# TensorE's product with w3 ahead of the values' product in six of eight slots of an attention and mixture-of-experts kernel

## The chip, the cores and the metric

One core of a Trainium2 chip runs the whole program. The metric is the device time of one execution in microseconds (us). TensorE (PE in the rows, with PEld for its weight loads), VectorE (DVE), ScalarE (ACT), GpSimd (POOL) and SyncE (SP, which only issues DMAs) each run a queue of their own, in order, and wait for each other on semaphores.

## The reference

For each of 8 batches, `x` is 256 x 128. All is in float32.

```python
def layer(x, ctx):                                   # x: (8, 256, 128), ctx: (8, 256, 64)
    n = layernorm(x)
    q, k, v = heads(n @ Wq + bq), heads(n @ Wk + bk), heads(n @ Wv + bv)     # 16 heads of 8
    y = softmax(causal(q @ k.T / sqrt(8))) @ v
    qc, kc, vc = heads(n @ Wcq + bcq), heads(ctx @ Wck + bck), heads(ctx @ Wcv + bcv)
    y = y + softmax(qc @ kc.T / sqrt(8)) @ vc
    x = x + merge(y) @ Wp + bp
    f = layernorm(x)
    shared = (silu(f @ w1.T) * (f @ w2.T)) @ w3s.T                           # hidden width 512
    scores = sigmoid(f @ router.T)
    gates = scores * top2_mask(scores + expert_bias)                         # 8 experts
    h1, h2 = split(einsum('td,ehd->teh', f, w12))                            # hidden width 128 each
    return x + shared + einsum('teh,edh->td', silu(h1) * h2 * gates, w3)
```

## The kernel before, in words

A batch's attention is cut into 8 *units*, each of 4 heads: units 0 to 3 are the causal self-attention, units 4 to 7 the attention to the context. A unit's softmax goes in four steps. TensorE computes the scores a first time, in two halves (`maxima`, lines 471, 472 and 476), and VectorE reduces them to maxima (lines 1057 and 1063). TensorE transposes the maxima into the bank Y (`shift_rows`, line 549) and VectorE subtracts them from the queries (`qs`, line 1030). TensorE computes the shifted scores in two halves (`exp_pass`, lines 458 and 460) and ScalarE exponentiates them into `probs` (line 816). Last comes the *values' product* (`values`, line 582), 16 matmuls of `vs` with `probs` into Y, which ScalarE copies into `yT` (line 803).

The feed-forward part is cut into 6 *pairs* of chunks (2 pairs of the shared expert, 4 of the routed ones). For a pair TensorE computes h1 into bank A and h2 into bank Bk (`hidden`, line 434, which is also the line of other products), ScalarE takes the tanh (`th`, line 796), VectorE makes `act` (line 939) and `hid` (`times_h2`, line 948, which reads h2 out of Bk). Then comes the *product with w3* (`w3_product`, line 434, `Bk<-w3T,hid`, 8 matmuls), written over h2 in Bk, and VectorE adds the result to `acc` (`add_up`, lines 963 and 979).

The program is written out in turns. Turn t runs t from -1 to 7 through 8 *slots*, and a written-out list (`DRAIN`) of what is left follows. Slot s of a turn works on several units at once: the exponential pass is that of unit s, `shift_rows` that of the next unit, `maxima` that of the unit after, `values` that of the unit before. Six slots also carry a pair of an earlier batch:

```python
def pair_of(s):
    return {5: (0, -1), 6: (1, -1), 0: (2, -2), 1: (3, -2), 2: (4, -2), 3: (5, -2)}.get(s)
```

The second number says how many turns back the pair's batch lies. So turn 1 has pairs in slots 5 and 6 only, and turns 2 to 7 have them in all six: 38 in the turns and 10 in the drain, which calls `values` and `w3_product` from its own list.

What happens in a slot with a pair, in the order of each engine's queue:

- TensorE: exponential pass half 0, half 1 (which wait for the reduced maxima of the next unit, half 0 and half 1, since they write over those scores), h1, h2, an early use of bank Cb, `shift_rows`, maxima half 0 and half 1 (which wait for ScalarE's exponentials of the slot, half 0 and half 1), then the two products in question, then a late use of bank Cb. The late uses are `tokens2` in slot 0 (transposes of `yT`, line 665, which wait for the copy of unit 7 that the same slot's values' product feeds), the q and k projections in 1, the output projection in 2, `x2T` in 3, `cT` in 4 (a slot with no pair), the router in 5, none in 6 and `tokens1` in 7 (no pair either). In slots 3 and 4 short matmuls that only keep TensorE busy (`fill`, line 490) stand ahead of the exponential passes.
- VectorE: `act`, `qs` of the next unit (waits for `shift_rows`), `hid`, the maxima half 0 and half 1, `add_up` (waits for the product with w3), and what it has to do for bank Cb.
- ScalarE: exponentials half 0, the tanh, exponentials half 1, what it has to do for the early use of Cb, the copy to `yT` (waits for the values' product), the late use of Cb.

`values` waits for Y to be free, which it is when VectorE has finished `qs`, and for `probs`. `w3_product` waits for `hid`.

Of the kernel before, what the change touches and what calls it, by code (L numbers as in the profile page):

```python
# [45 lines left out]
def values_of(s):  # L46
    return ((s - 1) % SLOTS, 0 if s > 0 else -1)


def pair_of(s):  # L50
    return {5: (0, -1), 6: (1, -1), 0: (2, -2), 1: (3, -2), 2: (4, -2), 3: (5, -2)}.get(s)


def h1_of(s):

    return {4: (0, -1), 5: None, 7: (2, -1), 0: None}.get(s, pair_of(s))
# [78 lines left out]
def wait(eng, sem, n):  # L135

    if not isinstance(n, int) or n > 0:
        eng.wait_ge(sem, n)
# [20 lines left out]
def attention_moe_program(nc, x, ctx_in, Wk, bk, Wq, bq, Wv, bv, Wck, bck, Wcq, bcq, Wcv, bcv, Wp, bp,  # L159
                          w12, w3, shared_w1, shared_w2, shared_w3, router_w, expert_bias, out):  # L160
    with ExitStack() as stack:
# [162 lines left out]
        def wait_bank(eng, turn, uses, free, name):  # L324

            found, wrapped = turn.users_before(uses, name)
            if uses is C_USES and turn.at(-1):
                found = found[1:2]
            elif uses is C_USES and turn.at(0) and wrapped:
                found = found[0:2]  # L330
            else:
                found = found[0:1]
            for before, off in found:
                s, part, of = free[before]
                wait(eng, s, turn.n(off, part, of))
# [12 lines left out]
        def raw_banks(turn, s):  # L348

            if turn.at(0):  # L350
                return [s] if s < SLOTS - 1 else []
            return [SLOTS - 1 + s] if turn.at(1) and SLOTS - 1 + s < RAW_BANKS else []
# [77 lines left out]
        def _(pe):  # L430
            def parts(dst, pairs_):

                for i, (a, m) in enumerate(pairs_):
                    mm = nc.tensor.matmul(dst, a, m, start=(i == 0), stop=(i == len(pairs_) - 1))  # L434
                return mm
# [51 lines left out]
            def fill(bank, n):  # L487

                for _ in range(n):
                    nc.tensor.matmul(bank[:, 0:T], ident_bf[:, :], causal[:, :].unsqueeze(1).broadcast_to([P, 2, P]),  # L490
                                     start=True, stop=True)
# [13 lines left out]
            def exp_pass(turn, s):  # L505

                if turn.has(0):
                    for half in range(2):
                        if half == 0:

                            wait(pe, shifted[s], turn.n(0))
                        keep_warm(turn, s, WARM_EXP)
                        un, on = shift_of(s)
                        if turn.has(on):

                            wait(pe, reduced[un], turn.n(on, half + 1, 2))
                        else:
                            wait(pe, exped[s - 1], turn.n(0, half + 1, 2))
                        exp_scores(s, half).then_inc(scores[s], 1)

            def hidden(turn, pair, w, i=0):

                p, o = pair
                if w == 0 and p == 0:
                    wait(pe, x2T_hi, turn.n(o))
                    wait(pe, x2T_lo, turn.n(o))
                if w == 0 and p == 0 and turn.at(1):
                    pe.wait_ge(raw_hi, RAW_BANKS)
                    pe.wait_ge(raw_lo, PAIRS)
                if w == 1 and i == 0:  # L530

                    if p > 0:
                        wait(pe, summed[p - 1], turn.n(o, SUM_STEPS[p - 1], SUM_STEPS[p - 1]))
                    elif turn.loop or turn.t + o > 0:
                        wait(pe, summed[PAIRS - 1], turn.n(o - 1, SUM_STEPS[-1], SUM_STEPS[-1]))
                bank = pair_banks[i % SETS][w]
                for c in range(2):
                    mm = parts(bank[:, c * T:(c + 1) * T],
                               three(w12_hi[:, p, w, c, :], w12_lo[:, p, w, c, :], x2T[:, 0, :], x2T[:, 1, :]))
                mm.then_inc(ffn[p], 1)  # L540

            def shift_rows(turn, s):

                u, o = shift_of(s)
                if turn.has(o):
                    wait(pe, reduced[u], turn.n(o, 2, 2))
                    wait_bank(pe, turn, Y_USES, y_free, f"shift{u}")
                    for qt in range(NT):
                        mm = nc.tensor.transpose(Y[:, qt * P:(qt + 1) * P], shifts[:, qt, :], ident[:, :])  # L549
                    mm.then_inc(shift_T[u], 1)  # L550
# [17 lines left out]
            def values(turn, s):  # L568

                u, o = values_of(s)  # L570
                if turn.has(o):
                    wait_bank(pe, turn, Y_USES, y_free, f"value{u}")
                    wait(pe, exped[u], turn.n(o, 2, 2))
                    if u < NG:
                        wait(pe, masked[u], turn.n(o))
                    kind, g = divmod(u, NG)
                    if g == 0:
                        wait(pe, v_ready[kind], turn.n(o))
                    for kt in range(NT):
                        for j in range(GH):  # L580
                            q0 = P * kt if kind == 0 else 0
                            mm = nc.tensor.matmul(Y[QUAD * j:QUAD * (j + 1), q0:T], vs[:, kind, kt, GH * g + j, :],  # L582
                                                  probs[u % 2][:, j, kt * T:(kt + 1) * T - q0],
                                                  start=(kt == 0), stop=(kt == NT - 1))
                    mm.then_inc(valued[u], 1)

            def w3_product(turn, pair, i=0):

                p, o = pair
                wait(pe, hid_ready[p], turn.n(o))  # L590
                bank = pair_banks[i % SETS][1]
                if p < SHARED_PAIRS:
                    for tt in range(NT):
                        mm = parts(bank[:, tt * P:(tt + 1) * P],
                                   [(hid[i % SETS][:, c, tt * P:(tt + 1) * P], w3T[:, 2 * p + c, :]) for c in range(2)])
                else:
                    for c in range(2):
                        for tt in range(NT):
                            k = c * NT + tt
                            mm = parts(bank[:, k * P:(k + 1) * P],  # L600
                                       [(hid[i % SETS][:, c, tt * P:(tt + 1) * P], w3T[:, 2 * p + c, :])])
                mm.then_inc(ffn[p], 1)
# [81 lines left out]
            def one_turn(turn):  # L684
                for s in range(SLOTS):
                    exp_pass(turn, s)
                    if pair_of(s):
                        if h1_of(s) and turn.has(h1_of(s)[1]):
                            hidden(turn, h1_of(s), 0)
                        if s == 6:  # L690
                            bank_c(turn, EARLY[s])
                        if turn.has(pair_of(s)[1]):
                            hidden(turn, pair_of(s), 1)
                        if turn.at(1) and s == 2:

                            fill(Bk, 3)
                        if s != 6:
                            bank_c(turn, EARLY[s])
                        shift_rows(turn, s)
                        for half in range(2):  # L700
                            maxima(turn, s, half)
                        values(turn, s)
                        if turn.has(pair_of(s)[1]):
                            w3_product(turn, pair_of(s))
                    else:
                        shift_rows(turn, s)
                        maxima(turn, s, 0)
                        if turn.has(h1_of(s)[1]):
                            hidden(turn, h1_of(s), 0)
                        bank_c(turn, EARLY[s])  # L710
                        maxima(turn, s, 1)
                        values(turn, s)
                    for i in raw_banks(turn, s):
                        raw_bank(i)
                    bank_c(turn, LATE[s])

            def drain(turn):
                for step, i in DRAIN:
# [18 lines left out]
                    elif step == "bank_c":  # L737
                        bank_c(turn, (i, -1))

            turns(pe, one_turn, drain)  # L740


# [482 lines left out]
```

## Time and profile before

| | |
|---|---|
| time before, median of 3 runs | 424.03 us (423.29 to 424.42) |
| the profiled execution, its own time | 421.15 us |
| its span in the trace | 419.4 us |
| TensorE busy (matmuls) | 385.7 us, 92% |
| TensorE's weight loads | 291.9 us, 70% |
| VectorE busy | 352.0 us, 84% |
| ScalarE busy | 197.4 us, 47% |
| GpSimd busy | 77.5 us, 18% |
| DMA | 47 GB/s on average |

The span is the stretch that the trace covers; 1.7 us of the execution's time lie outside it. Times in the rows are microseconds from the start of the span. The end of a matmul in the trace is modelled, so the starts are the safer numbers. A bracket behind a row gives the idle time of the engine just before it and who ended it.

### The profile page before, as it was taken

To read this page: it belongs to the slowest core of one execution; us is meant where nothing else is said; L and a number is where in the kernel's file an instruction comes from. 1 tells how busy PE (TensorE), PEld (TensorE's weight loads), DVE (VectorE), ACT (ScalarE), POOL (GpSimd) and SP (SyncE) were. 2 spreads that over 40 slices of the span, in tenths; PEclk is the share of its full clock that TensorE was granted. 3 is DMA by queue.
4 is the path that set the end of the run, shared out by engine and by line. 5 is a ranking of instruction groups with operands and counts; after the bars stand their busy time and mean duration, and the time that the engine had idled before them with its cause. 6 is when DMAs were issued, how large, how long until landed. Compare 5 with 4: busy or idle time off the path is not lost.

```text
span 419.4 us, 10085 instructions
## 1 busy us (share of the span) xinstructions
PE 385.7 (92%) x3724; PEld 291.9 (70%) x3724; DVE 352.0 (84%) x1186; ACT 197.4 (47%) x326; POOL 77.5 (18%) x140
## 2 busy tenths in 40 slices
PE   1569999999999999999999999999999999999996
PEld 0446666667687767867687767867787767767895
DVE  4487777787999889998999889988999789884897
ACT  5125655555453554554454554554454554455221
POOL 5012101312122012212132013212131103201210
PEclk9999999999999999999999999999999999999999
DMA  5721102010201102110111101110201101000000
GB/s 129 222 101 45 65 19 90 34 45 20 71 19 58 52 20 70 52 46 12 65 33 52 52 33 57 59 52 2 77 15 45 45 33 46 2 27 1 2 15 13
DMA packets 28496, 19.87 MB, mean 47 GB/s; under 512 B 6680, under 2 KB 26272, under 8 KB 28448
## 3 DMA queue, kind: packets, MB, share of 16 engines
q1 hardware_dynamic: 27296, 19.02, 14.0%
q8 instruction: 30, 0.49, 0.5%
q10 hardware_dynamic: 1152, 0.20, 0.3%
q14 instruction: 18, 0.15, 0.1%
HBM read 5.58 MB, written 1.05 MB: 16 GB/s over the span
## 4 chain that ended last, share of the span: by engine, by line
PE 62%; DVE 26%; issue 6%; ACT 2%; DMA 2%; SPq 1%; DVEq 0%; ACTq 0%
PE Bk L434 12%; PE Y L582 9%; PE A L434 8%; DVE shifts L1063 7%; PE S L458 7%; PE Cb L434 7%; DVE masked_s L1057 5%; PE S L476 3%; PE Y L549 3%; PE Cb L665 3%; PE S L471 2%; DVE hid L948 2%; DVE act L939 2%; PE S L460 2%; DVE acc L979 2%
## 5 line engine op out<-in xcount | busy, mean ns | idle before, releaser
L816 ACT ACTIVATE probs<-S 128x1024 f32<-128x1024 f32 (+1 forms) x128 | 114.1, 916 | 45.6 <-PE S L460 44.8
L1057 DVE CUSTOM_DVE_ANT_0 masked_s<-S,later_keys 128x256 f32<-128x256 f32 (+1 forms) x256 | 74.1, 353 | 5.1 <-PE S L472 4.9
L1063 DVE TENSOR_REDUCE shifts<-S 128x4 f32<-128x1024 f32 x64 | 75.4, 1217 | 0.9 <-PE S L476 0.5
L803 ACT COPY yT<-Y 128x256 f32<-128x256 f32 x64 | 23.8, 373 | 94.6 <-PE Y L582 94.6
L582 PE MATMUL Y<-probs,vs 128*32 128x256 f32 (+1 forms) x1024 | 62.4, 361 | 3.9 <-DVE qs L1030 2.9
L1113 POOL TENSOR_SCALAR_AFFINE_SELECT probs<-probs 128x1024 f32<-128x1024 f32 x32 | 35.2, 1101 | 154.0 <-ACT probs L816 154.0
L458 PE MATMUL S<-qs,qk 32*128 32x256 f32 x256 | 45.4, 387 | 7.7 <-DVE shifts L1057 4.5
L434 PEld LDWEIGHTS Bk<-w3T,hid 128*128 128x128 f32 x336 | 40.7, 191 | 12.6 <-DVE hid L948 8.5
L434 PE MATMUL Bk<-w3T,hid 128*128 128x128 f32 x336 | 48.4, 287 | 0.6 <-DVE hid L948 0.6
L582 PEld LDWEIGHTS Y<-probs,vs 128*32 128x32 f32 x1024 | 26.9, 110 | 25.4 <-DVE qs L1030 8.8
L1030 DVE TENSOR_TENSOR qs<-qk,Y 128x256 fp32r<-128x256 f32 x64 | 26.6, 415 | 18.5 <-PE Y L549 18.5
L458 PEld LDWEIGHTS S<-qs,qk 32*128 32x128 f32 x256 | 22.9, 184 | 25.8 <-issue 8.6
L939 DVE SCALAR_TENSOR_TENSOR act<-th,A 128x512 f32<-128x512 f32 x42 | 28.7, 683 | 11.7 <-ACT th L796 11.1
L796 ACT ACTIVATE th<-A 128x512 f32<-128x512 f32 x42 | 25.2, 599 | 24.6 <-PE A L434 24.5
L434 PE MATMUL A<-x2T,w_hi 128*128 128x256 f32 x168 | 36.1, 307 | 0.0
L434 PE MATMUL Bk<-x2T,w_hi 128*128 128x256 f32 x168 | 34.0, 295 | 0.0
L979 DVE SCALAR_TENSOR_TENSOR acc<-Bk,gates,acc 128x128 f32<-128x128 f32 x112 | 31.3, 341 | 0.2 <-PE Bk L434 0.2
L460 PE MATMUL S<-qs,qk 32*128 32x128 f32 (+1 forms) x256 | 30.5, 249 | 0.0
L549 PE MATMUL Y<-ident,shifts 128*128 128x128 f32 x128 | 26.9, 292 | 2.6 <-DVE shifts L1057 2.6
L948 DVE TENSOR_TENSOR hid<-act,Bk 128x512 f32<-128x512 f32 x42 | 28.6, 681 | 0.5 <-PE Bk L434 0.4
L434 PEld LDWEIGHTS A<-x2T,w_hi 128*128 128x128 f32 x168 | 25.4, 188 | 4.2
L434 PEld LDWEIGHTS Bk<-x2T,w_hi 128*128 128x128 f32 x168 | 25.6, 188 | 2.6 <-issue 0.4
(149 smaller groups left out, 679.8 us busy)
## 6 DMA issues: line engine op xcount, KB each, us to landing
qk<-nat SPq DMA_DIRECT2D x192, 64.0 KB, 1.9
xin<-in_x_dram SPq DMA_DIRECT2D x8, 128.0 KB, 2.3
w_raw<-in_L_ffn_w_dram SPq DMA_DIRECT2D x4, 256.0 KB
xres<-in_x_dram SPq DMA_DIRECT2D x8, 128.0 KB, 2.4
out_dram<-acc SPq DMA_DIRECT2D x8, 128.0 KB, 1.8
cin<-in_ctx_dram SPq DMA_DIRECT2D x8, 64.0 KB, 2.1
w_raw<-in_L_ffn_shared_w_dram SPq DMA_DIRECT2D x4, 128.0 KB
w_raw<-in_L_ffn_w_dram SPq DMA_DIRECT2D x1, 512.0 KB
```

The source lines that it names most:

```text
L434: mm = nc.tensor.matmul(dst, a, m, start=(i == 0), stop=(i == len(pairs_) - 1))
L458: nc.tensor.matmul(S[:, j, 0:T], qk[r, u, 1, 0:P], qs[r, u % 2, :], start=True, stop=True)
L460: mm = nc.tensor.matmul(S[:, j, T:2 * T - q0], qk[r, u, 1, P:T], qs[r, u % 2, q0:T], start=False, stop=True, skip_group_check=True)
L549: mm = nc.tensor.transpose(Y[:, qt * P:(qt + 1) * P], shifts[:, qt, :], ident[:, :])
L582: mm = nc.tensor.matmul(Y[QUAD * j:QUAD * (j + 1), q0:T], vs[:, kind, kt, GH * g + j, :], probs[u % 2][:, j, kt * T:(kt + 1) * T - q0], st ...
L816: nc.scalar.activation(probs[s % 2][:, hs, 0:kept(s)], S[:, hs, 0:kept(s)], ACT.Exp, scale=SCALE).then_inc(exped[s], 1)
L939: nc.vector.scalar_tensor_tensor(out=act1[i % SETS][:, :], in0=th[i % SETS][:, :], scalar=1.0, in1=pair_banks[i % SETS][0], op0=ALU.add, o ...
L948: nc.vector.tensor_tensor(hid[i % SETS][:, :, :].rearrange("p c t -> p (c t)"), act1[i % SETS][:, :], pair_banks[i % SETS][1], ALU.mult).t ...
L979: nc.vector.scalar_tensor_tensor(out=acc[:, tt, :], in0=bank[:, k * P:(k + 1) * P], scalar=gates[:, tt, e:e + 1], in1=acc[:, tt, :], op0=A ...
L1057: r_ = nc.vector.tensor_tensor_reduce(out=masked_s[:, j, T - q * T:T - q * T + keys], in0=S[:, j, T - q * T:T - q * T + keys], in1=later_k ...
L1063: nc.vector.tensor_reduce(dst.rearrange("p q j -> p j q"), S[:, hs, :].rearrange("p j (q k) -> p j q k", q=NT), AX_X, ALU.max).then_inc(re ...
L1113: return nc.gpsimd.affine_select(out=dst, in_=dst, compare_op=compare, fill=fill, base=base, pattern=pattern, channel_multiplier=step)
```

## The change

In the six slots with a pair, the two calls at the end of the slot's TensorE work trade places. The drain's list and all other engines' queues stay as they are.

```diff
@@ one_turn of TensorE
                         shift_rows(turn, s)
                         for half in range(2):
                             maxima(turn, s, half)
-                        values(turn, s)
                         if turn.has(pair_of(s)[1]):
                             w3_product(turn, pair_of(s))
+                        values(turn, s)
                     else:
                         shift_rows(turn, s)
                         maxima(turn, s, 0)
```

## Rows read from the trace of the kernel before

**Rows 1.** Busy time by engine in one whole turn.

```profile
232.79:279.64 46.85, 45.65 (x464) 34.85 (x460) 42.42 (x147) 23.36 (x39) 9.09 (x15) 1.00 0.14 45
```

**Rows 2.** The chain of work that ended last, slots 1 to 3: start, us, what.

```profile
261.38 1.09 PE Bk L434 x8
...
271.63 0.83 PE Cb L434 x6
```

**Rows 3.** Timeline, end of slot 5 and start of slot 6.

```profile
236.50 0.68 DVE L948 TENSOR_TENSOR hid<-act,Bk 128x512 f32<-128x512 f32 x1
236.63 1.07 PE L582 MATMUL Y<-probs,vs 128*32 128x256 f32 x16
239.89 0.19 PEld L458 LDWEIGHTS S<-qs,qk 32*128 32x128 f32 x2 [0.30 <-DVE shifts L1063]
```

**Rows 4.** Timeline, end of slot 6 and start of slot 7.

```profile
243.71 0.68 DVE L948 TENSOR_TENSOR hid<-act,Bk 128x512 f32<-128x512 f32 x1
243.84 1.07 PE L582 MATMUL Y<-probs,vs 128*32 128x256 f32 x16
245.93 0.39 PE L458 MATMUL S<-qs,qk 32*128 32x256 f32 x2
246.48 1.94 ACT L816 ACTIVATE probs<-S 128x1024 f32<-128x1024 f32 x2 [1.13 <-PE S L460]
247.65 0.33 PE L471 MATMUL S<-qk 32*128 32x128 f32 x2
```

**Rows 5.** Timeline, end of slot 0 and start of slot 1.

```profile
253.64 0.68 DVE L948 TENSOR_TENSOR hid<-act,Bk 128x512 f32<-128x512 f32 x1
253.94 1.07 PE L582 MATMUL Y<-probs,vs 128*32 128x256 f32 x16
254.94 1.16 PE L434 MATMUL Bk<-w3T,hid 128*128 128x128 f32 x8
255.07 0.37 ACT L803 COPY yT<-Y 128x256 f32<-128x256 f32 x1 [1.36 <-PE Y L582]
255.93 0.60 PE L665 MATMUL Cb<-ident,yT 128*128 128x128 f32 x4
256.92 0.19 PEld L458 LDWEIGHTS S<-qs,qk 32*128 32x128 f32 x2 [0.16 <-DVE shifts L1057]
```

**Rows 6.** Timeline, the two products of slot 1.

```profile
260.39 0.68 DVE L948 TENSOR_TENSOR hid<-act,Bk 128x512 f32<-128x512 f32 x1
260.53 0.86 PE L582 MATMUL Y<-probs,vs 128*32 128x256 f32 x16 [0.35 <-DVE qs L1030]
```

**Rows 7.** Timeline, the two products of slot 2.

```profile
266.31 0.68 DVE L948 TENSOR_TENSOR hid<-act,Bk 128x512 f32<-128x512 f32 x1
266.54 0.86 PE L582 MATMUL Y<-probs,vs 128*32 128x256 f32 x16
```

**Rows 8.** Timeline, end of slot 3 and start of slot 4.

```profile
273.21 0.68 DVE L948 TENSOR_TENSOR hid<-act,Bk 128x512 f32<-128x512 f32 x1
273.35 0.86 PE L582 MATMUL Y<-probs,vs 128*32 128x256 f32 x16
276.21 2.09 ACT L816 ACTIVATE probs<-S 128x1024 f32<-128x1024 f32 x2 [0.29 <-PE S L460]
276.73 0.39 PE L458 MATMUL S<-qs,qk 32*128 32x256 f32 x2 [0.24 <-DVE shifts L1063]
277.53 0.51 PE L476 MATMUL S<-qk 32*128 32x256 f32 x4
```

**Rows 9.** Timeline, exponential pass half 1 of slot 2 in turn 7.

```profile
356.59 0.19 PEld L458 LDWEIGHTS S<-qs,qk 32*128 32x128 f32 x2 [0.64 <-DVE shifts L1057]
```

**Rows 10.** Costliest groups of the page: busy us, mean ns, idle before.

```profile
L979 DVE SCALAR_TENSOR_TENSOR acc<-Bk,gates,acc 128x128 f32<-128x128 f32 x112 | 31.3, 341 | 0.2 <-PE Bk L434 0.2
```

**Rows 11.** Timeline, a values' product of the first turn.

```profile
34.11 1.51 PE L582 MATMUL Y<-probs,vs 128*32 128x256 f32 x16
```

## The prediction

> **What bounds the kernel now.** I read the page first (TensorE 92% busy, VectorE 84%), then the windows of one turn, then the chain of waits, and last the timeline of that turn around each of the six slots with a pair.
>
> One turn lasts 46.85 us, in which TensorE is busy for 45.65 and VectorE for 42.42 [rows 1]. Neither has room to spare: TensorE's idle time comes in pieces of a few tenths of a microsecond. The reader is to see in the chain that it runs on TensorE without a break from the product with w3 of slot 1 to the early product of slot 3, 261.38 to 272.46 us (23 pieces, all PE) [rows 2]. What delays TensorE there delays the kernel in full. Elsewhere the chain passes to VectorE for a while (maxima, `qs`, `hid`) and back.
>
> The reader is to see in each slot's timeline which of two products could start first. VectorE makes `qs` and right behind it `hid`. The values' product starts as soon as `qs` is done (in slot 1 after 0.35 us idle for it [rows 6]), and runs while `hid` is being made. The product with w3 needs `hid`.
>
> **The change part by part.** No instruction is added or taken away: 16 matmuls of the values' product and 8 of the product with w3, with their weight loads, change order. No DMA moves, since neither product issues one, and POOL and SP wait for neither.
>
> *What gets sooner.* The product with w3 ends sooner by at most the length of the values' product. Its only reader is `add_up`, which stands behind two maxima in VectorE's queue. Its 112 instructions for the routed pairs had 0.2 us of idle time ahead of them in all, for TensorE [rows 10]. So there is 0.2 us to win at most, and I count nothing.
>
> *What gets later.* TensorE now stands at the product with w3 until `hid` is done, with the values' product queued behind it, which could have run. The delay in each slot is the end of `hid`, plus 0.05 us for the signal, less the time at which the values' product started before. The 0.05 is an estimate, from the 0.06 us between the modelled end of a values' product and the copy that waits for it (253.94 + 1.07 = 255.01, and 255.07 [rows 5]).
>
> - Slot 5: 236.50 + 0.68 + 0.05 - 236.63 = 0.60 us [rows 3]
> - Slot 6: 243.71 + 0.68 + 0.05 - 243.84 = 0.60 [rows 4]
> - Slot 0: 253.64 + 0.68 + 0.05 - 253.94 = 0.43 [rows 5]
> - Slot 1: 260.39 + 0.68 + 0.05 - 260.53 = 0.59 [rows 6]
> - Slot 2: 266.31 + 0.68 + 0.05 - 266.54 = 0.50 [rows 7]
> - Slot 3: 273.21 + 0.68 + 0.05 - 273.35 = 0.59 [rows 8]
>
> *What of it lies beside other work.* The delay is worth nothing where TensorE would have waited anyway before the next thing that counts.
>
> Slot 5: half 1 of the next exponential pass had 0.30 us of idle time before it, for VectorE's maxima [rows 3]. These run beside the products and don't get later. The delay is 0.60 - 0.30 = **0.30**.
>
> Slot 6: the late slot is empty, and the exponential pass comes next. ScalarE had been idle for 1.13 us when the scores of half 0 came, and its two exponentials took 1.94, so 0.97 each. Half 0 ended near 247.45, and the maxima of slot 7 started at 247.65 [rows 4], because they wait for it. So the delay goes scores, exponentials, maxima, and no slack takes from it: **0.60**.
>
> Slot 0: the delay of the product with w3 is 0.43, but the late use here is `tokens2`, which reads the `yT` that this slot's values' product feeds. Before, the product with w3 stood between, and the copy (255.07 to 255.44) was done before the transposes (255.93), hidden below it [rows 5]. That cover is gone. The product with w3 starts at 254.37 and has the 0.99 us from 254.94 to 255.93, so the values' product starts at 255.36. The copy starts 1.13 behind that start as before (253.94 to 255.07), at 256.49, takes 0.37, and with the signal the transposes start at 256.91 and not 255.93, 0.98 later. Half 1 of the next exponential pass had 0.16 us of idle time before it, for VectorE [rows 5]: **0.82**.
>
> Slots 1 and 2 lie in the unbroken stretch of TensorE [rows 2]: **0.59** and **0.50** in full.
>
> Slot 3: half 1 of the next pass stood 0.24 us idle for VectorE [rows 8], which would leave 0.35. But the exponentials of half 0 started 0.29 us after ScalarE went idle, for the scores, took 1.04 each and ended at 277.25; the maxima of slot 4 started at 277.53 [rows 8]. With 0.59 more they end at 277.84. From the end of such an exponential to the maxima I take 0.09 us, between the 0.05 of a signal and the 0.20 of slot 6 (247.45 to 247.65 [rows 4]), so the maxima start at 277.93: **0.40**.
>
> The sum of a turn is 0.30 + 0.60 + 0.82 + 0.59 + 0.50 + 0.40 = **3.21 us**. Turns 2 to 6 have all of it: 16.05. Turn 1 has slots 5 and 6: 0.90. In turn 7 the pass behind slot 1 had 0.64 us idle before it, for VectorE [rows 9], which covers slot 1's 0.59: 2.62. The drain's order doesn't change: nothing. Together 19.6 us.
>
> *Bounds of what the trace doesn't show.* No matmul of the values follows one with w3 in the trace, and none of an exponential pass follows one of the values. From one group to the next the shape of the weights changes three times in a slot, before as after, so I take zero. The two groups differ little in length, start to next start: 1.00 us for 16 matmuls of values, 0.99 for 8 with w3 [rows 5]. As bounds I take a tenth of that, 0.1 us less or more in each of 38 slots, 3.8 us both ways. The slacks may overlap or be used twice: without any of them (0.30 + 0.16 + 0.19 in a turn, and 0.64 once) the sum is 4 us larger.
>
> The profiled execution took 421.15 us, so it becomes 440.7. The median of the runs shown, 424.03, is 2.9 us above it, so the runs should show 443.6.
>
> **The rivals.**
>
> *VectorE takes it up.* VectorE is busy for 42.42 of 46.85 us of a turn [rows 1]. If it sets the pace in more places than I read, only the delays in the unbroken stretch and at the copy count: 0.82 + 0.59 + 0.50 = 1.91 a turn, 12 us in all, **436**. For it speaks the chain's passing to VectorE in slots 3, 5 and 6; against it, that its `qs` there waits for TensorE's transposes, so it gets later with them.
>
> *Everything adds.* No slack counts, and the changes of shape cost 0.1 us more in each slot: 19.6 + 4 + 3.8 = 27.4 us, **451**. For it speaks that a late TensorE also starts VectorE's next maxima late; against it, that the idle times in the rows are there.
>
> *Not slower.* The whole delay hangs on `hid` being ready after the maxima's last matmul. Were it ready before the values' product started, that is 0.43 to 0.60 us sooner against TensorE than in these rows, the product with w3 would fill the time in which TensorE stood for `qs` (0.35 us in slot 1 [rows 6]), and slots other than slot 0 would cost nothing or win. A point for it would be that the later TensorE gives VectorE time to catch up. But `qs` is released by TensorE's own transposes and `hid` follows it, so they move together. It would give 424 less 0.3 for each of 32 slots, more 0.5 for each of 6 slots 0 (the 0.98 less 0.43, for the copy): about **418**.
>
> *The clock falls.* The granted clock was 1.00 in the turn read (the level of 2.4 GHz), with TensorE idle for 1.2 us of 46.85 [rows 1]; now it is idle for 4.4. A values' product took 1.07 us in this turn [rows 3] and 1.51 in the first one [rows 11]. If that is what the lower level costs, a turn's 45.65 us of TensorE's work would take 64.4, and a single turn that ran so would add 19 us: **462** or more. Against it: the `fill` matmuls stay, and no single pause here is longer than about 1 us. The Trainium skill (TensorE: Matmul & The Clock Gate, A second HAM failure mode) reports a kernel whose clock swung between its two levels because TensorE paused briefly and often between groups of matmuls. This change adds just such pauses, so by that rule this rival would be the likelier one; the trace shows short pauses in every slot and a clock that stayed up.
>
> **How the numbers follow.** My sum, 0.66, with 439 to 448 as its own range; VectorE takes it up 0.12; everything adds 0.14; not slower 0.04; the clock 0.04. The predicted time is 443.6 us. The range of 434 to 452 holds the first three, and leaves out the last two and the far ends. The runs of the kernel before lie 1.1 us apart, about 0.3%, so that much is what can be told from no change. Slower by more than that has 0.96; faster and within it share the case of not slower, 0.02 each.
>
> **What would show it.** In the profile after, the product with w3 should stand idle for `hid` (line 948) before its first matmul, on PE and not on PEld alone, some 0.5 to 0.8 us in nearly every slot: more than 15 us over the run, where the values' product had its small waits for `qs`. The transposes `Cb<-ident,yT` of slot 0 should wait 0.5 us for ScalarE's copy. A turn should last 50.1 us. `add_up` should start as soon behind the maxima as before. The prediction is wrong if a turn stays under 48 us, if the maxima's reductions start no later against the turn than now, or if the granted clock leaves 1.00.

## The result, and the profile after

The changed kernel takes 446.01 us (median of 5 executions, 442.94 to 454.25), against 424.03 us before (423.29 to 424.55): 1.052 times as long, with a 95% interval of 1.048 to 1.056. That is 22.0 us slower, where 19.6 were forecast, and inside the range.

Some executions of every kernel here, the one before included, have a mean granted clock below 0.998 and are 2 to 15 us longer than the others. So I compare two other numbers beside the medians. The first are the executions with a mean of 0.998 or more ("at full clock"): 442.94 and 443.31 us for the changed kernel, and 421.06 to 421.62 for the kernel before, taken beside the later experiments, so +21.8 us. The second is the length of one turn in the trace. The trace of the changed kernel is that of the execution of 454.25 us. Its granted clock was at the lower level in two stretches, of which the later one ends at 117.2 us, and stood at 1.00 in turns 2 to 7, which lie behind that.

The windows of one whole turn of the changed kernel, against [rows 1]:

```profile
223.88:274.22 50.34, 45.37 (x460) 34.17 (x460) 42.89 (x148) 22.99 (x39) 9.17 (x15) 1.00 0.13 44
```

The turn is 50.35 us long and not 46.85: 3.50 more, where the sum said 3.21. TensorE's busy time is about what it was (45.65 us before, 45.37 now), so its idle time has grown from 1.2 us to 5.0. The clock stayed at 1.00.

The page's costliest groups name the place; the second row answers to [rows 10]:

```profile
L434 PE MATMUL Bk<-w3T,hid 128*128 128x128 f32 x336 | 50.3, 294 | 23.8 <-DVE hid L948 23.6
...
L979 DVE SCALAR_TENSOR_TENSOR acc<-Bk,gates,acc 128x128 f32<-128x128 f32 x112 | 31.4, 344 | 0.2 <-PE Bk L434 0.2
```

TensorE stood 23.6 us for `hid` ahead of the product with w3, and `add_up` waits for TensorE exactly as long as before, 0.2 us. So what the swap makes sooner, nobody had waited for.

The timeline of the changed kernel at the ends of slots 5, 6, 0, 1, 2 and 3, against [rows 3 to 8]. The bracket is the idle time before, and who ended it.

```profile
259.12 1.16 PE L434 MATMUL Bk<-w3T,hid 128*128 128x128 f32 x8 [0.59 <-DVE hid L948]
260.21 1.07 PE L582 MATMUL Y<-probs,vs 128*32 128x256 f32 x16
...
266.55 1.16 PE L434 MATMUL Bk<-w3T,hid 128*128 128x128 f32 x8 [0.67 <-DVE hid L948]
...
277.07 1.16 PE L434 MATMUL Bk<-w3T,hid 128*128 128x128 f32 x8 [0.37 <-DVE hid L948]
278.15 1.07 PE L582 MATMUL Y<-probs,vs 128*32 128x256 f32 x16
279.29 0.37 ACT L803 COPY yT<-Y 128x256 f32<-128x256 f32 x1 [2.88 <-PE Y L582]
279.72 0.66 PE L665 MATMUL Cb<-ident,yT 128*128 128x128 f32 x4 [0.49 <-ACT yT L803]
...
284.50 1.16 PE L434 MATMUL Bk<-w3T,hid 128*128 128x128 f32 x8 [0.94 <-DVE hid L948]
285.59 0.86 PE L582 MATMUL Y<-probs,vs 128*32 128x256 f32 x16
286.38 0.50 PE L434 MATMUL Cb<-xT,wx_hi 128*128 128x256 f32 x2
...
291.10 1.16 PE L434 MATMUL Bk<-w3T,hid 128*128 128x128 f32 x8 [0.45 <-DVE hid L948]
...
298.70 1.16 PE L434 MATMUL Bk<-w3T,hid 128*128 128x128 f32 x8 [0.69 <-DVE hid L948]
```

All six places show the stand, 0.37 to 0.94 us. In slot 1 it was 0.35 for `qs` before [rows 6], and is 0.94 for `hid` now: 0.59 more, as worked out. In slot 0 the second stand is there too, 0.49 us for the copy of `yT`. One number is new: from the first matmul with w3 to the first of the values it takes 1.09 us (259.12 to 260.21, and 284.50 to 285.59), where w3's 8 matmuls and the group behind them were 0.99 apart in slot 0 before [rows 5], and 0.92 in slot 1:

```profile
261.31 1.16 PE L434 MATMUL Bk<-w3T,hid 128*128 128x128 f32 x8
262.23 0.48 PE L434 MATMUL Cb<-xT,wx_hi 128*128 128x256 f32 x2
```

To place the loss, I took the start of half 1 of each exponential pass (the fifth of a pass's eight weight loads `S<-qs,qk`) and the distance from one pass to the next. "Slot 0" is the distance from the pass of slot 0 to that of slot 1, and holds slot 0's two products. One turn, in us:

| slot | 0 | 1 | 2 | 3 | 4 | 5 | 6 | 7 | turn |
|---|---|---|---|---|---|---|---|---|---|
| before | 5.38 | 6.42 | 6.21 | 7.17 | 3.99 | 6.03 | 6.77 | 4.90 | 46.87 |
| after | 6.16 | 6.99 | 6.95 | 7.60 | 4.13 | 6.35 | 6.69 | 5.48 | 50.35 |

Turns 2 to 6 of the kernel before are 46.80 to 46.87 us long by this reading. I go on with the 46.85 of [rows 1], so a difference of turns is good to about 0.03 us. Part of slot 3's delay comes out one slot later (in 4), and all of slot 6's (in 7), by way of ScalarE's exponentials.

### The profile page after: what moved, and what is told of

It reads as the page before. It is cut to its first block, busy times and chain, and to the rows that moved or that the text cites. A ratio compares the mean times of both kernels' runs of the same rounds, so it can differ in the third digit from the quotient of the medians.

```text
span 452.5 us, 10085 instructions
## 1 busy us (share of the span) xinstructions
PE 396.5 (88%) x3724; PEld 296.6 (66%) x3724; DVE 355.0 (78%) x1186; ACT 195.7 (43%) x326; POOL 77.8 (17%) x140
## 3 DMA queue, kind: packets, MB, share of 16 engines
HBM read 5.58 MB, written 1.05 MB: 15 GB/s over the span
## 4 chain that ended last, share of the span: by engine, by line
PE 61%; DVE 23%; ACT 6%; issue 6%; DMA 2%; SPq 1%; DVEq 0%; ACTq 0%
PE Bk L434 15%; PE Y L582 12%; PE Cb L434 8%; PE A L434 6%; DVE hid L948 6%; PE S L458 5%; DVE masked_s L1057 4%; DVE act L939 3%; ACT probs L816 3%; PE S L476 2%; PE Y L549 2%; PE Cb L665 2%; ACT th L796 2%; PE S L460 2%; DVE qs L1030 1%
## 5 line engine op out<-in xcount | busy, mean ns | idle before, releaser
L434 PE MATMUL Bk<-w3T,hid 128*128 128x128 f32 x336 | 50.3, 294 | 23.8 <-DVE hid L948 23.6
L582 PE MATMUL Y<-probs,vs 128*32 128x256 f32 (+1 forms) x1024 | 65.0, 374 | 0.0
L434 PEld LDWEIGHTS Bk<-w3T,hid 128*128 128x128 f32 x336 | 42.3, 197 | 31.9 <-DVE hid L948 31.8
L458 PE MATMUL S<-qs,qk 32*128 32x256 f32 x256 | 38.9, 395 | 3.8 <-DVE shifts L1057 2.7
L434 PE MATMUL Bk<-x2T,w_hi 128*128 128x256 f32 x168 | 35.1, 302 | 0.0
L796 ACT ACTIVATE th<-A 128x512 f32<-128x512 f32 x42 | 25.1, 598 | 19.6 <-PE A L434 18.9
L458 PEld LDWEIGHTS S<-qs,qk 32*128 32x128 f32 x256 | 19.9, 189 | 20.7 <-issue 14.8
L476 PE MATMUL S<-qk 32*128 32x256 f32 x256 | 26.3, 336 | 0.7 <-ACT probs L816 0.2
```

Source lines behind the costliest of these rows:

```text
L458: nc.tensor.matmul(S[:, j, 0:T], qk[r, u, 1, 0:P], qs[r, u % 2, :], start=True, stop=True)
L476: mm = nc.tensor.matmul(S[:, j, q * T:(q + 1) * T], qk[r, u, 0, q * P:(q + 1) * P], qk[r, u, 1, :], start=(q == 0), stop=True, skip_group_ ...
L796: nc.scalar.activation(th[i % SETS][:, :], pair_banks[i % SETS][0], ACT.Tanh, scale=0.5).then_inc(ffn_th[p], 1)
```

## The experiments

Each kernel has the same work as the kernel before, in another order. The turn is read from the trace as in the table above, in turn 4.

### The swap in slot 0 alone

```diff
-                        values(turn, s)
+                        if s != 0:
+                            values(turn, s)
                         if turn.has(pair_of(s)[1]):
                             w3_product(turn, pair_of(s))
+                        if s == 0:
+                            values(turn, s)
```

> The product with w3 stands ahead of the values' product in slot 0 alone (6 places). The copy theory: slot 0 pays twice, for the wait on hid and for the copy to yT that is no longer hidden below the product with w3, 0.82 us a turn, so 424.0 + 4.9 = 428.9 us, and the transposes Cb<-ident,yT wait some 0.5 us for the copy. Rival, only the wait on hid costs: 0.43 - 0.16 = 0.27 a turn, 425.6. Rival, VectorE sets the pace there: 424.

Measured: 429.25 us (427.57 to 431.74, clock 0.980 to 0.995; none at full clock), a ratio of 1.011 with an interval from 0.998 to 1.023, which alone decides nothing. The turn decides: 47.57 us, so 0.72 more than before (0.79 more in slot 0, and 0.10 less in slot 1). That is near the copy theory (0.82), and neither 0.27 nor nothing. The timeline of this kernel at the end of slot 0:

```profile
215.10 1.16 PE L434 MATMUL Bk<-w3T,hid 128*128 128x128 f32 x8 [0.37 <-DVE hid L952]
216.19 1.07 PE L582 MATMUL Y<-probs,vs 128*32 128x256 f32 x16
217.32 0.37 ACT L807 COPY yT<-Y 128x256 f32<-128x256 f32 x1 [2.89 <-PE Y L582]
217.75 0.31 PEld L665 LDWEIGHTS Cb<-ident,yT 128*128 128x128 f32 x3 [0.97 <-ACT yT L807]
217.75 0.44 PE L665 MATMUL Cb<-ident,yT 128*128 128x128 f32 x2 [0.49 <-ACT yT L807]
```

The copy now lies between the two TensorE groups, with nothing beside it.

### The swap everywhere but in slot 0

The same diff with the two conditions turned round (`s == 0` and `s != 0`).

> The swap in slots 5, 6, 1, 2 and 3, and the old order in slot 0. My sum without slot 0: 19.6 - 4.9 = 14.7, so 438.7 us, with stands of 0.5 to 0.7 us before the product with w3 for hid. If slot 0 is what carries the loss (its copy), 428 or less. If delays add up or cancel between slots, this and the run with slot 0 alone won't sum to the whole loss of some 19 to 22 us.

Measured: 440.13 us (438.27 to 444.95); at full clock 438.27 and 438.53, so 17.1 us more than before, where 14.7 were expected. The turn is 49.64 us, 2.79 more. With slot 0's 0.72 that makes 3.51, the whole change's 3.50. So slot 0's loss and that of the others add up and neither hide nor feed each other, and it is the other slots' terms, not slot 0's, that were too small in sum.

### Slots 1 and 2; slots 3, 5 and 6

The same diff with `s in (1, 2)` and with `s in (3, 5, 6)`.

> The swap in slots 1 and 2 alone (12 places), where the chain of the kernel before ran on TensorE without a break. The wait for hid alone: 0.59 + 0.50 = 1.09 us a turn, less slot 1 in the last turn: 5.9 us. With a cost of the order itself, seen in the changed kernel's trace (1.09 us from the first matmul with w3 to the first of the values, against 0.92 to 0.99 from w3's first to that of the group behind it before), 0.1 to 0.17 more in each: 7.3 us over a run of before at full clock. Rival, VectorE sets the pace: 2 us or less.

> The swap in slots 3, 5 and 6 (20 places), where TensorE had idle time for VectorE behind the products. My sum with slack taken off: 0.40 + 0.30 + 0.60 a turn, 8.7 us in all, and with 0.17 for the order in slots 3 and 5 some 10.5 us. Rival, everything adds (no slack counts): 20 times 0.60, with the order's cost 14 us. Rival, VectorE takes it up: 4 us or less.

Measured for slots 1 and 2: 429.99 us (428.70 to 439.57; ratio 1.014, 1.010 to 1.018); at full clock 428.70 and 428.83, and a turn of 48.24, 1.39 more. None of the executions of the kernel before beside these two kernels was at full clock, so I set their times against the 421.06 to 421.62 of the other experiments: 7.4 us more. That is the wait plus the cost of the order (7.3), and more than the wait alone (5.9). The turn says it more firmly, since the wait alone would have been 1.09. For slots 3, 5 and 6: 432.13 us (430.50 to 441.69; ratio 1.019, 1.015 to 1.023); at full clock 430.50 and 431.22, 9.2 to 9.9 more, and a turn of 48.21, 1.36 more. That lies between my sum with and without the order's cost (8.7 and 10.5). Both rivals fall: slack counts (not 14), and VectorE doesn't take the delay up (not 4). The two turns add to 2.75, against 2.79 for the five slots together.

### VectorE makes `hid` ahead of `qs`, in the changed kernel and in the one before

```diff
+                    if pr and turn.has(pr[1]):
+                        times_h2(turn, pr)
                     u, o = shift_of(s)
                     if turn.has(o):
                         ...
                         nc.vector.tensor_tensor(qs[:, u % 2, :], ...)
-                    if pr and turn.has(pr[1]):
-                        times_h2(turn, pr)
```

> The changed kernel, and VectorE makes hid ahead of qs instead of behind it (no work added). The theory that TensorE's wait for hid is the loss: hid is ready 0.4 us sooner, or in slot 5 a whole microsecond, and the stands shrink from about 0.6 us to 0 to 0.3, so the time falls by more than half of the loss, to 427 to 434 us; slot 0 keeps its wait for the copy. Rival, the order itself costs on TensorE (a change of shape of weights between the groups, 0.1 us or more in each place): the time stays at 440 or above though the waits for hid are gone.

> The control: the kernel before with VectorE making hid ahead of qs. By the wait theory now the values' product stands for qs, which comes 0.4 to 0.68 us later in every slot but 5, so this is slower than before by some 10 to 18 us (434 to 442). If making hid first is good or bad by itself for another reason (VectorE's maxima), it would show here too: a time below 424 would say that the gain of the run beside it is not the wait for hid.

Measured for the changed kernel with `hid` first: 431.72 us (428.69 to 435.74; ratio 1.016, 1.011 to 1.021), 428.69 to 429.65 at full clock, and a turn of 48.10. No work was taken away and TensorE's new order stayed, only the wait got shorter, and 2.25 of the turn's 3.50 us are gone. The rival, that the order itself costs nearly all, falls. The timeline shows what is left in slot 2:

```profile
225.60 0.69 DVE L952 TENSOR_TENSOR hid<-act,Bk 128x512 f32<-128x512 f32 x1
226.21 0.41 DVE L1037 TENSOR_TENSOR qs<-qk,Y 128x256 fp32r<-128x256 f32 x1
226.35 1.16 PE L434 MATMUL Bk<-w3T,hid 128*128 128x128 f32 x8 [0.24 <-DVE hid L952]
```

The product with w3 starts while VectorE is still at `qs`, after 0.24 us and not 0.45.

The control, the kernel before with `hid` first, took 432.24 us (431.01 to 444.74; ratio 1.016, 1.003 to 1.029), 431.01 and 431.55 at full clock, and a turn of 48.34. Its table of waits has the mirror image of the stand (us in total, times, longest):

```profile
PE Y L582 <- DVE qs L1033: 20.6, 32, 1.5
```

TensorE stood 20.6 us for `qs` ahead of the values. So the direction is as expected: the product that goes first must be the one whose operand VectorE makes first. The size was not: 9.8 us at full clock lies just below the 10 to 18 expected. Slots 5 and 6 had got shorter by 0.47 and 0.26 us (5.56 and 6.51), which I had not counted. That pointed to the experiment with `hid` first in slot 5.

### The same, with slot 0 left as it was before

`hid` first and the swap, both with the condition `s != 0`.

> The changed kernel with hid made ahead of qs, but both orders of before in slot 0. The copy theory: slot 0's transposes no longer wait for the copy, which takes 0.5 us or more off each of 6 turns: 424 to 426 us at full clock against 428.7 with slot 0 changed. If slot 0 costs nothing once hid is early, 428.7 stays.

Measured: 427.48 us (426.41 to 432.90; ratio 1.007, 1.001 to 1.013), 426.41 to 426.51 at full clock. It is 2.2 us below the kernel with slot 0 changed; the turn is 47.67, 0.43 less: slot 0 is 0.54 shorter (5.37 against 5.91) and slot 1 0.11 longer. So the swap in slot 0 costs something even when `hid` is early, as the copy theory says. Its absolute time lies 0.4 us above what I expected.

### TensorE's late use of bank Cb ahead of the products

The third way to take the wait away: let TensorE do other work meanwhile, with VectorE's order untouched. First in the kernel before, in slot 1 only; then in slots 1, 2 and 5, with the swap everywhere; then with the swap in these three slots only.

```diff
+                        if late_first:                      # s == 1, or s in (1, 2, 5)
+                            bank_c(turn, LATE[s])
                         ...
-                    bank_c(turn, LATE[s])
+                    if not late_first:
+                        bank_c(turn, LATE[s])
```

> The kernel before with the q and k projections of slot 1 ahead of both products. They don't depend on qs, so TensorE has work in the 0.35 us in which it stood for qs there. The theory that order counts by what TensorE has ready: 0 to 0.3 us less in each of 5 or 6 turns, so 419.5 to 421 at full clock. If a change of shape between the groups eats it, no change or up to 1 us slower.

> The changed kernel with the late use of bank Cb (the q and k projections, the output projection, the router) ahead of both products in slots 1, 2 and 5. VectorE's order is not touched, so hid comes no sooner; TensorE has 0.45 to 0.9 us of other work while it is made. The wait theory: the stands for hid in these slots shrink to 0 to 0.15 us, and the turn falls from 50.35 to some 48.9 us, the whole by about 9 us, to 434 at full clock. Rival, the order's change of shapes is the loss: the turn stays above 50.

> Slots 1, 2 and 5 with the late use of bank Cb first, then the product with w3, then the values' product; slots 0, 3 and 6 as before. If both waits (for qs and for hid) are hidden and only the shapes cost 0.1 to 0.17 us a slot: a turn of 46.7 to 47.3 us against 46.85, 420 to 424 us at full clock. Under 46.8 it would beat the kernel before.

`late_first` took 428.69 us (426.00 to 431.51; ratio 1.012, 1.006 to 1.018), with the clock at 0.980 to 0.992 in all its executions; the turn is 46.84, the same as before. The 0.35 us of slot 1 weren't won:

```profile
267.19 0.47 PE L434 MATMUL Cb<-xT,wx_hi 128*128 128x256 f32 x2
...
268.06 0.86 PE L582 MATMUL Y<-probs,vs 128*32 128x256 f32 x16
268.85 1.16 PE L434 MATMUL Bk<-w3T,hid 128*128 128x128 f32 x8
269.94 0.39 PE L458 MATMUL S<-qs,qk 32*128 32x256 f32 x2
```

The product with w3 now has the exponential pass behind it, 1.09 us after its start, where the projections had come after 0.92. This order, too, has one change of weight shape more than the order before (four and not three, counted further down). From the first matmul of the maxima to the next exponential pass it took 3.44 us, where it had been 3.51, and half 1 of that pass came 0.07 us later behind half 0, so that nothing was left.

`late_first_after` took 452.91 us (450.96 to 463.77; ratio 1.072, 1.065 to 1.079), and its turn is 51.12 and not 48.9. I was wrong on the total, but the slots tell two things apart. Slot 1 went from 6.99 to 6.31 and slot 2 from 6.95 to 6.48. In `late_first_three`, where slot 0 is as before, they are 6.40 and 6.48 against 6.42 and 6.21 before. So slot 1's loss is gone in full and slot 2's by 0.47 of 0.74. This order takes away two things at once: the wait, which now has other work under it, and the added change of weight shape, since the late use and the product with w3 stand together again. It doesn't tell their shares apart. Slot 5 went the other way, to 8.26 and to 6.72 us:

```profile
255.28 0.35 PE L434 MATMUL Cb<-router_hi,x2T 128*128 128x8 f32 x2 [1.05 <-DVE vs L904]
...
255.94 1.83 PE L434 MATMUL Bk<-w3T,hid 128*128 128x128 f32 x8
257.70 1.94 PE L582 MATMUL Y<-probs,vs 128*32 128x256 f32 x16
```

The router's product needs bank Cb, which VectorE gives back only when it has made `vs`, and `vs` stands behind `hid` in its queue. I had overlooked that wait: instead of hiding the one for `hid`, the move put a longer one, 1.05 us, in its place. What it did to the clock stands further down. `late_first_three` took 434.29 us (431.77 to 438.39; ratio 1.028, 1.021 to 1.035), with a turn of 47.67 where 46.7 to 47.3 were expected, and is slower than the kernel before.

### `hid` first in slot 5 of the kernel before

The diff of above with the condition `s == 5`, and no swap.

> The kernel before with one thing changed: in slot 5 VectorE makes hid ahead of qs. There VectorE stood idle for 1.02 us before qs with act and h2 ready, so hid costs qs nothing, and the maxima behind it start up to 0.6 us sooner, for which the next exponential pass waited 0.30 us. With hid first in all slots the interval of slot 5 was 5.56 us against 6.03. If that gain belongs to slot 5 itself: a turn of 46.4 to 46.6 us instead of 46.85, some 2 us less in all. If it was only time borrowed from the slots before, the turn stays at 46.85.

Measured: 421.33 us (417.84 to 431.80) against 423.37 beside it, a ratio of 0.991 (0.986 to 0.997); at full clock 417.84 to 418.29 against 421.18 to 421.62, 3.4 us less, where some 2 were expected. The turn is 46.23 us, 0.62 less (46.4 to 46.6 were expected), of which slot 5 gives 0.48. In the kernel before VectorE had stood idle in slot 5 ahead of `qs`:

```profile
236.16 0.42 DVE L1030 TENSOR_TENSOR qs<-qk,Y 128x256 fp32r<-128x256 f32 x1 [1.02 <-PE Y L549]
```

With `hid` moved into this gap, the timeline is:

```profile
233.69 0.69 DVE L948 TENSOR_TENSOR hid<-act,Bk 128x512 f32<-128x512 f32 x1 [0.24 <-PE Bk L434]
234.48 0.42 DVE L1033 TENSOR_TENSOR qs<-qk,Y 128x256 fp32r<-128x256 f32 x1
...
234.95 1.07 PE L582 MATMUL Y<-probs,vs 128*32 128x256 f32 x16
235.21 2.35 DVE L1066 TENSOR_REDUCE shifts<-S 128x4 f32<-128x1024 f32 x2
237.61 0.40 PE L458 MATMUL S<-qs,qk 32*128 32x256 f32 x4
```

The maxima follow `qs` after 0.73 us, where 1.33 us lay between the two starts before (236.16 to 237.49), and the exponential pass no longer waits for them: its four matmuls stand in one row. This version is faster than both kernels, if only by 0.9% than the one before.

### The swap from turn 2 on

```diff
-                        values(turn, s)
+                        if turn.t < 2:
+                            values(turn, s)
                         if turn.has(pair_of(s)[1]):
                             w3_product(turn, pair_of(s))
+                        if turn.t >= 2:
+                            values(turn, s)
```

> The change from turn 2 on, with turn 1's two places in the old order. By the sum of the turns 0.8 to 0.9 us less than the change in full: 442.1 at full clock, and the same turns of 50.35 us. If the swap in turn 1 is what lowers the granted clock between 93 and 117 us, this kernel shows no fall there in its runs; if the falls come without it too, as in the other kernels, the swap is not their cause.

Measured: 442.24 us (441.86 to 450.05; ratio 1.047, 1.041 to 1.053), 441.86 to 442.34 at full clock, against 442.94 and 443.31 for the change in full: turn 1's two places cost 0.6 to 1.5 us, with 0.90 worked out. The trace of the swap in slots 3, 5 and 6 gives them more closely: 0.80 us in slots 5 to 7 of turn 1. The turn is 50.33. Its profiled execution had no fall of the clock, but one execution of 450.05 us had a mean of 0.994, as three executions of the kernel before did beside it. And the swap in slot 0 alone, which changes nothing before turn 2, had falls at 54.9, 72.0 and 89.1 us, ahead of its first swapped product. In the changed kernel itself the longest fall began at 93.3 us, while its first swapped product starts at 101.75. So the swap doesn't bring the falls about. Whether it made that one last longer isn't settled.

## Why the prediction was right, point by point

The slots can be measured closer, from the first matmul of a slot's maxima. In the table, "first product" is how much later than before the first of the two products starts, "next pass" how much later the next exponential pass starts (half 0), and "caught up" how much closer half 1 of that pass follows half 0. The control is the kernel before with `hid` first: it has the waits too, but the old order. All are means of turns 2 to 6, in us.

| slot | changed kernel: first product | next pass | caught up | control: first product | next pass |
|---|---|---|---|---|---|
| 0 | 0.44 | 1.15 | 0.36 | 0.51 | 0.51 |
| 1 | 0.60 | 0.79 | 0.13 | 0.60 | 0.60 |
| 2 | 0.57 | 0.76 | 0.00 | 0.69 | 0.69 |
| 3 | 0.60 | 0.75 | 0.31 | 0.60 | 0.60 |
| 5 | 0.60 | 0.79 | 0.49 | 0.00 | 0.00 |
| 6 | 0.60 | 0.60 | 0.60 | 0.45 | 0.45 |

In the control the delay of the first product is passed on as it is. In the changed kernel it grows by 0.15 to 0.19 us on the way in slots 1, 2, 3 and 5, and not in slot 6. With `hid` first in the changed kernel, where the waits are shorter, it still grows by 0.15 to 0.20 in slots 1, 2, 3 and 5 and by nothing in slot 6.

- **Who waits for whom: right.** TensorE stands for `hid` in all six places and `qs` is no longer waited for. One experiment shortened the wait and left TensorE's new order as it was: `hid` first gave back 2.25 of 3.50 us a turn.
- **Nothing won from the earlier product with w3: right.** 0.2 us of waiting in `add_up`, before and after.
- **Slot 0, 0.82 a turn: 0.72 measured** by itself. The two parts, `hid` and the uncovered copy, are both in the trace (0.37 and 0.49 us). That the size fits is in part luck: the next pass was delayed by 1.15 us and not by 0.98, and its half 1 caught up 0.36 and not 0.16.
- **Slots 1 and 2, 0.59 and 0.50: 0.66 and 0.73 measured** with the swap in these two alone, 0.30 more a turn. This is the term that was mis-sized: "From one group to the next the shape of the weights changes three times in a slot, before as after, so I take zero." It doesn't change as often before as after. The rows give the shapes: 32 rows for the maxima and the exponential pass (`32*128`), 32 columns for the values (`128*32`), full width for w3 and for every late use of Cb (`128*128`). Before, w3 and the late use stood together, which makes three changes from the maxima to the next pass; now the values stand between them, which makes four. Slot 6 has no late use and three changes in both kernels, and there nothing is added. So the term is 0.15 to 0.19 us in each of slots 1, 2, 3 and 5. My choice of zero was wrong, and so was my bound of 0.1 us a slot. Slots 1 and 2 show it most, because little or nothing is caught up behind them.
- **Slot 2 has another, smaller part.** The chain of work of the changed kernel passes through ScalarE there, which no step of mine had:

```profile
287.74 0.47 ACT nat L782
288.20 0.70 ACT probs L816
288.91 0.49 ACT th L796
289.43 0.54 DVE act L939
289.96 0.07 issue
290.03 0.41 DVE qs L1030
290.44 0.61 DVE hid L948
291.05 0.04 issue
291.10 1.16 PE Bk L434 x8
```

  Each row is start, length and what. ScalarE comes later to `th`, so VectorE to `act` and `hid`: with `hid` on the path, its operands count too. Before, the chain ran on TensorE here [rows 2]. It can't be more than the 0.07 us by which the first product's 0.57 exceeds the 0.50 worked out; most of the rest (0.19) comes behind that product.
- **Slots 3, 5 and 6, 1.30 together: 1.36 measured.** That slack takes off part of the delay was right, and slot 3's and 6's loss comes by way of the exponentials. That the sum fits so well is luck again. Slot 3 lost 0.57 us with what comes out in slot 4 (0.40 worked out), and slots 5 and 6 lost 0.82 with what comes out in slot 7 (0.90 worked out). Slot 5's own 0.32 is the delay of 0.79 less the 0.49 caught up, where I had 0.60 less 0.30.
- **Turn 7, 2.62: 3.4 measured.** Slot 1 is covered in full there, as [rows 9] said (6.32 before and after). The rest is more than in a whole turn: 0.93 in slot 0, and 0.58 and 0.60 in slots 5 and 6. Behind these three slots half 1 of the pass follows half 0 after 0.11 us in turn 7, before as after, so there nothing is caught up.
- **The sum: 19.6 against 21.8 at full clock.** Five turns at 3.50, 3.4 in turn 7 and 0.8 in turn 1 make 21.7.
- **The rivals.** VectorE doesn't take it up (slots 3, 5 and 6 alone cost 9.2 us). Not everything adds; that rival's sum was too low besides, since without any slack it is 4.8 us more and not 4 (0.65 in six turns, 0.30 in turn 1 and 0.59 in turn 7). `hid` doesn't come earlier against TensorE by itself. The clock did not fall in turns 2 to 7 of the changed kernel's trace, with 5.0 us of short pauses a turn. By the Trainium skill (TensorE: Matmul & The Clock Gate, A second HAM failure mode) brief and frequent pauses let the clock swing between its levels; this trace does not agree with that, while `late_first_after`, below, whose clock fell once in each of five turns, does. The price that the prediction set on such a fall was too low: at the lower level a values' product took 1.94 us in `late_first_after`, and not 1.51.

## What to carry to other kernels

When two groups of an in-order queue are to trade places, look up when each one's operand is made, and by whom: here the better order on TensorE was the one in which VectorE produces, and what is won by the earlier result is worth only what its reader had waited. Count the changes of weight shape in both orders, with the groups on either side. Then look at what each group had hidden (here a copy of 0.37 us), and what each has to wait for in its new place (the bank that a third engine still reads). The cheapest gain was on the other engine: an operation that was ready moved into a gap in which its engine stood idle.

## What the runs showed of the hardware

- **The clock can fall in a turn with short stands only.** In `late_first_after` the granted clock fell once in each of turns 2 to 6, each time in slot 5. Windows: before, in and after one fall.

```profile
201.60:205.00 3.40, 2.35 (x25) 2.00 (x24) 2.43 (x5) 0.92 (x2) 0.00 (x0) 1.00 0.14 40
205.00:208.40 3.40, 3.40 (x24) 1.96 (x23) 2.38 (x7) 0.00 (x0) 0.00 (x0) 0.50 0.02 5
208.40:211.80 3.40, 3.40 (x32) 2.81 (x28) 1.18 (x3) 3.21 (x7) 2.22 (x6) 1.00 0.00 0
```

  TensorE had been busy for 2.35 of 3.40 us, with the 1.05 us stand in it, when the clock went from 2.4 to 1.2 GHz. At that level the 8 matmuls with w3 took 1.83 us instead of 1.16, and the 16 of the values 1.94 instead of 1.07. Slot 5 took 8.26 us, against 6.72 in `late_first_three`, which has the same order there and no fall: 1.5 us lost for each. But `late_first_three` has the same stand in slot 5 (1.08 us), and its clock stayed at 1.00:

```profile
244.20:247.60 3.40, 2.32 (x25) 1.98 (x24) 2.36 (x5) 0.97 (x2) 0.00 (x0) 1.00 0.17 42
```

  So this stand alone doesn't bring the fall. `late_first_three` has fewer stands in the other slots; whether that is what kept its clock up isn't shown.
- **A change of weight shape costs time on TensorE.** Eight 128x128 products took 0.9 to 1.0 us to the next group when that had full-width weights, and 1.09 us when it had 32-column or 32-row weights. One change more between the maxima and the next pass cost 0.15 to 0.20 us in all, in two kernels, and the control with the old order had none of it.
- **Falls of the clock in the first 120 us differ from one execution of the same program to the next.** The kernel before had a mean clock from 0.976 to 1.000 and took from 421.06 to 435.64 us beside the first four kernels. Where its clock fell isn't on record, since its traced execution had no fall. In the traces of the other kernels all falls but those of `late_first_after` in slot 5 lay between 41 and 117 us. Nothing here explains when they come.
